# Products without a use on TensorE between attention and experts, two tiles finished in halves, and one transpose group moved ahead of the last logits

## What is computed

```python
mod = (_silu(c) @ wmod).reshape(8, 6, 1, -1)           # sa, ca, ga, sb, cb, gb
h = layernorm(x) * (1 + ca) + sa
x = x + ga * attention(h)                               # 16 heads of 8, causal
h = layernorm(x) * (1 + cb) + sb
logits = h @ Wr + br;  topv, topi = top_k(logits, 2);  gates = softmax(topv)
rank = cumsum(sel) - sel                                # place of a token in its expert's buffer
keep = rank < 1024                                      # 8 experts, capacity 1024 each
out_e = gelu(xg_e @ W1_e + b1_e) @ W2_e + b2_e          # 1024 x 128 -> 512 -> 128
x = x + gb * sum over the 2 experts of gate * out_e
```

## Time and profile before

| | us |
|---|---|
| three executions | 534.47, 533.13, 530.73; median 533.13 |
| the profiled execution | 534.96 |
| its span, first to last instruction | 533.2 |

### The profile page before, as it was taken

One profiled execution on the slowest core, in us unless ns is written; L12 is line 12 of the kernel. 1 busy time (PEld: TensorE's weight loads), 2 busy tenths in 40 slices (PEclk: granted clock), 3 DMA queues, 4 the chain that ended last, 5 costly groups with the idle time before them and its releaser, 6 DMA issues.

```text
span 533.2 us, 11163 instructions
## 1 busy us (share of the span) xinstructions
PE 481.3 (90%) x3562; PEld 268.1 (50%) x3562; DVE 376.8 (71%) x1307; ACT 281.4 (53%) x527; POOL 331.9 (62%) x618
## 2 busy tenths in 40 slices
PE   7699998999999999999999999988489999999920
PEld 3234344355455445454554554444348677777720
DVE  3489988689989999999999999733353234333353
ACT  2400576567667677776776766765252434433300
POOL 5330454445757867867867877696418888775560
PEclk9979999899999999999999999999579999999985
DMA  3688968548656456556454340431563366553069
GB/s 91 184 209 219 292 214 221 152 154 226 174 138 195 141 173 192 153 177 181 112 150 137 90 121 11 121 90 58 163 192 104 127 186 179 167 149 107 1 198 313
DMA packets 70929, 83.49 MB, mean 157 GB/s; under 512 B 8330, under 2 KB 59303, under 8 KB 68438
## 3 DMA queue, kind: packets, MB, share of 16 engines
q1 hardware_dynamic: 51894, 59.60, 39.8%
q10 hardware_dynamic: 13856, 15.15, 8.8%
q0 software_dynamic: 5120, 8.04, 4.6%
HBM read 44.79 MB, written 35.80 MB: 151 GB/s over the span
## 4 chain that ended last, share of the span: by engine, by line
PE 55%; DVE 23%; issue 8%; POOL 4%; DMA 4%; ACT 1%; POOLq 0%; SPq 0%; DVEq 0%; ACTq 0%
PE ps L755 10%; PE ps L775 10%; DVE ps L1164 10%; PE ps L628 8%; PE ps L680 8%; PE ps L653 7%; DVE negmax L1164 2%; DVE ln L1130 2%; POOL slots_dram L1637 2%; PE ps L634 2%; DVE negmax L1168 2%; PE ps L728 2%; PE ps L591 1%; PE ps L765 1%; DMA krows<-k_dram 1%
## 5 line engine op out<-in xcount | busy, mean ns | idle before, releaser
L932 ACT ACTIVATE prob<-ps 128x512 f32<-128x512 f32 (+1 forms) x352 | 181.4, 559 | 81.3 <-PE ps L653 70.0
L1164 DVE CUSTOM_DVE_ANT_0 ps<-ps,maskrow 128x512 f32<-128x512 f32 (+1 forms) x256 | 155.5, 635 | 17.8 <-PE ps L628 16.6
L1591 POOL TENSOR_SCALAR_AFFINE_SELECT prob<-prob 128x128 f32<-128x128 f32 (+2 forms) x308 | 104.0, 349 | 75.6 <-ACT prob L932 69.8
L628 PE MATMUL ps<-krows,qrows 72*128 72x128 bf16 (+3 forms) x512 | 131.0, 306 | 8.8 <-DMA krows<-k_dram 4.2
L653 PE MATMUL ps<-qrows,krows 75*128 75x128 bf16 (+3 forms) x512 | 126.7, 300 | 2.7 <-DMA qrows<-mT 2.5
L628 PEld LDWEIGHTS ps<-krows,qrows 72*128 72x128 bf16 x512 | 45.5, 99 | 84.9 <-DVE negmax L1164 47.2
L680 PE MATMUL ps<-prob,vpad 128*32 128x128 f32 (+3 forms) x1024 | 86.0, 444 | 0.0
L986 ACT ACTIVATE qrows<-ps,b_sb 128x512 f32<-128x512 f32 x64 | 43.6, 688 | 75.4 <-PE ps L755 73.8
L1650 POOL DMA_INDIRECT picks_dram<-qrows,dest x64 | 63.2, 987 | 25.9 <-DVE qrows L1392 14.0
L1637 POOL DMA_INDIRECT slots_dram<-rows,index x64 | 65.4, 1022 | 22.0 <-issue 15.7
L1168 DVE TENSOR_REDUCE negmax<-ps 128x2 f32<-128x512 f32 (+1 forms) x96 | 61.2, 681 | 5.0 <-PE ps L634 5.0
(11 more groups left out here) (145 smaller groups left out, 546.4 us busy)
## 6 DMA issues: line engine op xcount, KB each, us to landing
qrows<-q_dram SPq DMA_DIRECT2D x48, 192.0 KB
krows<-k_dram SPq DMA_DIRECT2D x48, 192.0 KB
slots_dram<-empty ACTq DMA_DIRECT2D x32, 258.0 KB, 4.2
krows<-slots_dram SPq DMA_DIRECT2D x16, 516.0 KB, 5.0
vpad<-in_w SPq DMA_DIRECT2D x30, 256.0 KB, 3.2
k_dram<-kpart SPq DMA_DIRECT2D x40, 128.0 KB, 2.0
rows<-modB SPq DMA_DIRECT2D x8, 512.0 KB, 4.3
picks_dram<-zeros ACTq DMA_DIRECT2D x8, 512.0 KB
```

What stands on the lines that cost most here:

```text
L628: last = mm(bank[:, i * w:(i + 1) * w], qrows[0:SROWS, b % 2, h, qb * P:(qb + 1) * P], krows[0:SROWS, b % 2, h, 0:w], start=(i == 0), stop ...
L932: fn(prob[:, s % PRING, 0:w], ps[:, TB + ring(s, TRING), 0:w], ACT.Exp, scale=SCALE)\
L1164: nc.vector.tensor_tensor_reduce(ps[:, SB_ + ring(s, SRING), 0:w], ps[:, SB_ + ring(s, SRING), 0:w], maskrow[:, T - w:T], -1.0, -NEG, ALU. ...
L1591: sel_(out=blk, in_=blk, compare_op=ALU.is_ge, fill=0.0, base=0, pattern=[[0, nh], [1, P]], channel_multiplier=-1).then_inc(S["masked"], 1)
```

## The change

- `WARM_AT` gets five entries: 2, 4, 3, 20 and 3 idle products at x = 3, 8, 13, 25 and 40, all into bank 4.
- `slots_T(0)` on PE and `slots_copy(0)` on DVE go from x = 43 to x = 41, ahead of `logits` on PE and ahead of the first routing operation on DVE (both at 42).
- Tiles 13 and 14 are finished in two halves, each in a bank of its own ((5, 5, 7, 7) and (4, 4, 6, 6)), with a count on `y_mm` and one on `y_add` for each half; the last tile's quarters take banks 5, 7, 4, 6. The waits ahead of `down(15)` go, and single waits stand ahead of the halves and quarters that need them.

```diff
+def cuts(n):
+    return NT if n == 2 * E - 1 else 2 if n >= 2 * E - 3 else 1
+
+def parts_until(n, j):
+    return sum(cuts(i) for i in range(n)) + j * cuts(n) // NT + 1
...
-SLOT_T_AT = [43, 45, 57, 58, 67, 72, 73]
+SLOT_T_AT = [41, 45, 57, 58, 67, 72, 73]
...
-COPY_AT = [43, 52, 60, 61, 68, 71, 75]
+COPY_AT = [41, 52, 60, 61, 68, 71, 75]
...
-WARM_AT = []
+WARM_AT = [(3, 2), (8, 4), (13, 3), (25, 20), (40, 3)]
...
         def down_bank(n, j):
-            return (5, 6, 7, 4)[j] if n == 2 * E - 1 else 4 + n % 2
+            return {2 * E - 1: (5, 7, 4, 6), 2 * E - 2: (4, 4, 6, 6), 2 * E - 3: (5, 5, 7, 7)}.get(n, (4 + n % 2,) * NT)[j]
...
                 if n >= 2:
-                    pe.wait_ge(S["y_add"], n - 1)
+                    pe.wait_ge(S["y_add"], parts_until(n - 2, NT - 1))
                 for j in range(NT):
+                    if n == 2 * E - 3 and j == NT // 2:
+                        pe.wait_ge(S["r_carry"], B)
+                    if n == 2 * E - 2 and j == NT // 2:
+                        pe.wait_ge(S["slot_T"], 2 * E)
+                    if n == 2 * E - 1 and j >= NT // 2:
+                        pe.wait_ge(S["y_add"], parts_until(n - 1, 2 * j - NT))
...
-                    if n == 2 * E - 1 or j == NT - 1:
+                    if (j + 1) * cuts(n) % NT == 0:
                         last.then_inc(S["y_mm"], 1)
...
-                    pe.wait_ge(S["slot_T"], 2 * E)
-                    pe.wait_ge(S["y_add"], 2 * E - 1)
-                    pe.wait_ge(S["r_carry"], B)
...
             def add_bias_of(n, j):
-                dve.wait_ge(S["y_mm"], n + j + 1)
+                w = NT // cuts(n)
+                dve.wait_ge(S["y_mm"], parts_until(n, j))
...
-                tt(ysum[:, j], ps[:, down_bank(n, j), j * P:(j + 1) * P], b2_sb[:, TILES[n][0]], ALU.add)\
-                    .then_inc(S["y_add"], 1)
-                dve.wait_ge(S["y_add"], n + j + 1)
+                tt(ysum[:, j:j + w], ps[:, down_bank(n, j), j * P:(j + w) * P].rearrange("p (j c) -> p j c", j=w),
+                   b2_sb[:, TILES[n][0]:TILES[n][0] + 1, :].to_broadcast([P, w, C]), ALU.add).then_inc(S["y_add"], 1)
+                dve.wait_ge(S["y_add"], parts_until(n, j))
...
             def finish(n):
-                if n == 2 * E - 1:
+                if cuts(n) > 1:
                     dve.wait_ge(S[f"picked{n % 4}"], 16 * NT * (n // 4))
                     for j in range(NT):
-                        add_bias_of(n, j)
+                        if j * cuts(n) % NT == 0:
+                            add_bias_of(n, j)
                         gated(n, j)
```

More of the change, by code:

```diff
@@ L982, in gelu @@
                 if earlier(n, 2):
-                    act.wait_ge(S["y_mm"], n - 1)
+                    act.wait_ge(S["y_mm"], parts_until(n - 2, NT - 1))
                 for k in range(NF):
```

## The result

| | us |
|---|---|
| before | median 533.13 (530.73 to 535.69, 5 executions) |
| after | median 527.14 (526.15 to 528.29, 5 executions) |
| ratio after/before | 0.989, 95% interval 0.9859 to 0.9922 |
| profiled execution, before / after | 534.96 / 528.29 |
| span, before / after | 533.2 / 526.6 |

The forecast was 527.2. The profiled executions differ by 6.67 us, and the two traces can be split at four marks: the start of the last attention product (TensorE, the last of L690, L680 before), the start of `up(1)`, the start of `down(13)`, and the end.

A forecast was written before the change was run, and what follows sets the result against it. TensorE bounds the expert tiles; the half-clock gap before them and POOL's sends at the end were open. Gains of 4.4 and 1.6 us take 533.13 to 527.1, named 527.2 for crowding; range 524.5 to 531.0.

The forecast's parts named there:

- the two terms: Gain between attention and experts (the gap), 4.4 us, and gain at the kernel's end, 1.6 us.
- The idle products hold the clock: In the gap: products inside PE's waits prevent the fall to half clock, with 0 to 0.1 us of delay.
- Of the projection's gain only what POOL's pause allows arrives: Before `h2_T`: residual 0.86 us earlier, but deviation must wait for POOL's pause, so 0.6 us are left.
- The slots' load sets `slots_T(0)`, and the logits wait for it: In the gap: load lands after 3.9 us, at 383.5; logits start about 384.0, `up(0)` 2.5 us earlier.
- DVE's routing is late next: Ahead of `up(1)`: DVE's slot copy behind routing allows it at 390.4 instead of 394.80; PE would allow 389.5.
- The halves: At the end: tile 13's sends start 1.66 us earlier, the last four 1.5; gain 1.6 us, bounds 0 and 2.1.
- The sum: Whole kernel: 4.4 + 1.6 = 6.0 us gained, median 533.13 to 527.1, named 527.2 for crowding.
- the fall at 375.1 us: In the gap before the change: clock drops from 2.4 to 1.2 GHz at 375.1, until about 392.1.
- the sum for the end: Tiles 13 to 15: POOL's send times worked out from PE's finish plus DVE's bias add; gain 1.6 us.
- the clock falling again: Rival: clock falls while PE waits for tile 0's slots; gap gains 1.4 us, total 3.0, 530.1; chance 0.15.
- Late slots: Rival in the gap: tile 0's slots land up to 1 us later, 528.2; chance 0.1.
- The slower case: Rival: clock falls at 375.1, the 20 products run at half clock and delay `h2_T` 3.7 us; 535.0; chance 0.05.

The follow-up runs named there:

- e1: The changed kernel without any of its idle products: median 531.35 us, ratio to before 0.9952.
- e2: The changed kernel with slots_T(0) and slots_copy(0) put back at step 43: median 530.17 us, ratio to before 0.9935.
- e4: The changed kernel without the idle groups of 2, 4 and 3 products (x = 3, 8, 13): ratio to before 0.9891.
- e3: The changed kernel with tiles 13 and 14 finished whole instead of in halves: median 530.61 us, ratio to before 0.9947.
- e6: The changed kernel with slots_T(0) and slots_copy(0) back at step 43 and four more idle products at step 44: ratio to before 0.9887.
- e9: The changed kernel without the three idle products at x = 40: ratio to before 0.9931.
- e10: A second run of the changed kernel without the idle groups of 2, 4 and 3 products, on another chip: ratio to before 0.9883.
- e8: The changed kernel without POOL's pauses between the scatters of batch 6: median 540.35 us, ratio to before 1.0008.
- e11: The changed kernel with a third of the pause (128 instead of 384 columns) behind each scatter of batch 6: ratio to before 1.0003.
- e5: The changed kernel itself, measured again on a second chip: median 532.12 us, ratio to before 0.9878.
- e7: The changed kernel with 32 idle products instead of 20 at step 25: ratio to before 0.9918.

## Why the prediction was right

The time: 527.2 forecast, 527.14 measured, gain 6.0 forecast, 5.99 between the medians. Agreement to 0.1 us is luck: the interval of the measured gain is 4.2 to 7.5 us, and by stages the profiled pair gained 6.65 (4.72 and 2.42, less 0.49). What was right is the mechanism and the size of the two terms.

- **The idle products hold the clock.** Right: 1.00 all through the gap; without them (e1) the gap is 3.3 us longer. They fit into PE's waits as said: 0.20 us left ahead of L710 of the 1.07 before, and L719 no longer idle.
- **Of the projection's gain only what POOL's pause allows arrives.** Right: deviation directly behind the pause, `h2_T` 0.70 us earlier against the mark, for 0.6 forecast.
- **The slots' load sets `slots_T(0)`, and the logits wait for it.** Right: 0.96 us of idle time ended by the DMA. Its landing took 3.8 us for 3.9. `up(0)` came 2.68 us earlier for 2.5.
- **DVE's routing is late next.** Right: `up(1)` waited 0.73 us for the copy behind `top_slot`. The gain of the gap was 4.72 us for 4.4: 0.2 from `up(0)`, and 0.1 because the copy began beside the end of `top_slot` (389.79, for an end at 389.88).
- **The halves.** The start of tile 13's sends moved by 1.66 us, as worked out, in all four profiles with halves on the first chip; tile 15's first send came 1.48 us earlier for 1.5, after a wait of 0.65 us. The stage's gain in the first pair of profiles was 2.42 for 1.6. Four profiles with halves against two without give 1.7, e1, e2 and e4 against e3 1.3. The term's size was right there, and the surplus of the first pair (a last send of 1.05 us instead of 1.50, and 0.27 us less behind it) did not return.
- **The sum held in its parts**, with 0.49 us of a slower attention stage against it.

Three judgements behind the number were too sure. First, I took the fall at 375.1 us for a fixed feature of the kernel before. e1 and e4 show that, with the same waits unfilled, it may come later or not at all, and then most of the early groups' work is done for nothing. They may insure; in the totals they show nothing (ratio 0.9891 and 0.9883 without them, 0.9890 and 0.9878 with them). Second, the move. I put no number on it alone, and would have said 0.1 us (e2's expectation), while it is 0.8 (e6). It also closes PE's wait of 1.06 us in which e2 lost the clock. Third, the sum for the end lets DVE start as soon as PE is done. That held on the first chip (0.1 us); on the other two DVE was 3.9 to 5.3 us late at tile 14, and the start of tile 13's sends came 4.52 to 4.61 us after `down(13)` instead of 4.03. The forecast was not tried on a chip where this happens.

Of the rivals, the clock falling again was a real danger: it happened when the products at x = 40 (e9) or the move (e2) were taken away, for 1.2 and 1.8 us (the 1.8 with the move's own 0.8 in it), not 3.0. Both falls came at or behind the end of the logits and ended inside `up(0)`. Late slots did not happen. The slower case exists in its first half (e10) and does not reach its end, since the products themselves bring the clock back.

The Trainium skill (TensorE: Matmul & The Clock Gate, Part 4: PE-mode transpose) says that transposes do not count for the clock as products do. e9 fits: between its 20 products and the logits PE ran only transposes, and the clock fell. But e4 ran only transposes, and then the projection, for 4.8 us (369.35 to 374.15) and kept it, where e10 lost it after the same transposes. Neither that rule nor PE's busy time parts the two; what does is not shown.

Open: what holds the counts back in e8 and e11 and at the end of all profiles from e5 on, what the halves are worth on those chips, and how much of an execution's time without any fall in the gap the early groups save on average; the profiles show single executions.

## What to carry to other kernels

Split a long trace at marks that a change cannot touch and compare the stages: here totals of one kernel moved by 10 us and more on one chip, while the gap repeated within 0.11 us (19.09, 19.20 and 19.19 in after, e3 and e4) and showed parts worth 0.3 us. Repeat the stages on a second chip: the end stage came out 3 to 5 us longer there. A wait on TensorE in front of dense work can cost twice, once itself and once through the clock; idle products that lie wholly inside waits hold it, but count them against the instruction behind them: 12 more cost 1.3 us (e7). Before a pause is taken out of a queue of indirect DMAs, look at what waits for counts on other engines: it may be what lets them through. The same goes for a change that makes a queue of such DMAs unbroken, as the halves do.

## What was not expected of the hardware

- **Other engines' waits on PE ended late while POOL issued indirect DMAs.** With short breaks or none between the scatters, ACT was held for 5.5 us (e8) and 6.4 us (e11), until within 0.4 us of the load that waits for the last landing. With 0.44 us of break after each scatter the delay was under 0.1 us on one chip and 0.98 to 1.0 us on the others (e5: 370.58 to 371.56). In the unbroken sends at the end, 0.30 us apart, DVE was held for 3.9 to 5.3 us at tile 14 on those two chips and for 0.1 us on the first. What links the two is argued from the times; the profile names no cause.
- **The same kernel kept the clock in one execution and lost it in another.** 1.54 and 1.39 busy us of 4.10 were followed by no fall (e4) and a fall (e10). And a fall came after 2.93 busy us of 3.80 (e2).
- **Time at half clock goes with an execution's time.** From the mean clock c and the span, 2(1 - c) x span is the time at half clock. Among the 35 executions of the kernel before beside e1 to e4, the shortest (529.84 us) has a clock of 0.967 and a span of 528.1, 34.9 us at half; an ordinary one (534.89) 0.958 and 533.2, 44.8 us. Ten more microseconds at half clock went with five more of time. Over all 35 the two go together with a correlation of 0.83; that one causes the other is not shown.
